# Two sequences' q and k from one projection of 64-row weights, and the mix a pair later beside the output projection

## What is computed

```python
x = x + xattn0(layernorm(x), ctx)   # 8 heads of 8, softmax over |i-j| <= 64,
                                    # y = relu(attention @ w_out) * ctx, then y @ w_ct (the mix)
x = x + ffn0(layernorm(x))          # 256 x 256 ternary weight, scaled, norm clipped
x = x + xattn1(layernorm(x), ctx)   # q from x, k and v from ctx, rotary q and k, full softmax, out projection
x = x + ffn1(layernorm(x))          # 256 -> 1024 -> 256, 4-bit weights with low-rank additions
```

## Time and profile before

| what | value |
|---|---|
| median of 3 runs | 1358.52 us (1356.28 to 1361.82) |
| the profiled execution's own time | 1358.7 us |
| its span, first to last instruction | 1356.8 us |
| mean granted TensorE clock | 0.982 of full speed |
| busy in the span: PE, PEld, DVE, ACT, POOL | 94%, 63%, 68%, 63%, 52% |

### The profile page before, as it was taken

The page is one execution under the profiler, slowest core; times in us unless marked ns, Lnnn a source line. Parts: engine busy times, 40 slices in busy tenths (PEclk is TensorE's granted clock), DMA queues, the critical chain, the costliest instruction groups (busy, mean ns, idle before and its releaser), DMA issues.

```text
span 1356.8 us, 35892 instructions
## 1 busy us (share of the span) xinstructions
PE 1268.8 (94%) x10972; PEld 854.0 (63%) x10972; DVE 927.0 (68%) x2052; ACT 852.3 (63%) x1849; POOL 711.4 (52%) x1297
## 2 busy tenths in 40 slices
PE   6999999999999997868899999999999989999998
PEld 3677667777677764644566556666666646666665
DVE  6788888888888875549999978888888852111110
ACT  2576666666666765555888888888888772222111
POOL 4577778787777865045555656556655410100000
PEclk9999999999999999897999999999999999999999
DMA  8554444544445440023444434444444400000000
GB/s 202 117 132 102 114 113 112 111 109 111 111 102 120 100 96 7 12 52 92 90 99 102 105 88 100 97 102 110 98 97 102 105 6 0 31 16 15 15 15 31
DMA packets 90487, 113.33 MB, mean 84 GB/s; under 512 B 13972, under 2 KB 80276, under 8 KB 82740
## 3 DMA queue, kind: packets, MB, share of 16 engines
q1 hardware_dynamic: 89216, 111.25, 35.3%
q10 hardware_dynamic: 1206, 1.29, 0.4%
HBM read 18.66 MB, written 4.19 MB: 17 GB/s over the span
## 4 chain that ended last, share of the span: by engine, by line
PE 57%; POOL 16%; issue 10%; DVE 9%; ACT 3%; DMA 2%; POOLq 1%; SPq 0%; ACTq 0%; DVEq 0%
PE bank L475 9%; PE bank L435 8%; PE bank L678 8%; PE bank L669 8%; PE bank L451 8%; PE bank L433 5%; PE bank L487 4%; POOL probs L1340 4%; DVE row_max L1118 4%; POOL Qp L1311 2%; POOL rot L1322 2%; PE bank L627 1%; PE bank L507 1%; POOL k_rest L1327 1%; POOL q_rest L1307 1%
## 5 line engine op out<-in xcount | busy, mean ns | idle before, releaser
L1118 DVE TENSOR_REDUCE row_max<-bank 128x2 f32<-128x384 f32 (+1 forms) x1024 | 594.0, 616 | 109.9 <-PE bank L435 105.8
L714 ACT ACTIVATE probs<-bank 128x384 f32<-128x384 f32 (+1 forms) x1024 | 535.1, 542 | 182.9 <-PE bank L451 175.6
L435 PE MATMUL bank<-Ks,Qs 96*128 96x192 bf16 (+1 forms) x2048 | 372.2, 264 | 11.2 <-DMA Ks<-Ks 6.4
L451 PE MATMUL bank<-Qs,Ks 128*128 128x192 bf16 (+1 forms) x2048 | 366.0, 260 | 14.1 <-ACT probs L714 12.9
L1340 POOL TENSOR_SCALAR_AFFINE_SELECT probs<-probs 128x256 f32<-128x256 f32 (+1 forms) x512 | 260.9, 533 | 114.9 <-ACT probs L714 94.5
L435 PEld LDWEIGHTS bank<-Ks,Qs 96*128 96x128 bf16 x2048 | 187.9, 99 | 126.6 <-DVE row_max L1118 32.3
L475 PE MATMUL bank<-probs,V 128*32 128x192 f32 (+1 forms) x4096 | 248.2, 360 | 7.0 <-POOL probs L1340 5.7
L451 PEld LDWEIGHTS bank<-Qs,Ks 128*128 128x128 bf16 x2048 | 185.6, 97 | 48.2 <-ACT probs L714 34.5
L433 PE MATMUL bank<-band,ident 128*128 128x384 bf16 x512 | 168.7, 329 | 3.0 <-DMA Ks<-Ks 2.5
L475 PEld LDWEIGHTS bank<-probs,V 128*32 128x32 f32 x4096 | 107.4, 109 | 85.8 <-issue 43.9
L1277 DVE TENSOR_TENSOR X<-bank,X 128x256 f32 (+1 forms) x32 | 13.6, 424 | 185.6 <-PE bank L678 185.6
(11 more groups left out here) (118 smaller groups left out, 1675.3 us busy)
## 6 DMA issues: line engine op xcount, KB each, us to landing
Ks<-Ks SPq DMA_DIRECT2D x64, 576.0 KB
Qs<-Qs SPq DMA_DIRECT2D x128, 192.0 KB
Qs<-Qp SPq DMA_DIRECT2D x192, 64.0 KB
Ks<-Kp SPq DMA_DIRECT2D x192, 64.0 KB
side<-in_ctx SPq DMA_DIRECT2D x64, 128.0 KB, 2.1
X<-in_x SPq DMA_DIRECT2D x4, 1024.0 KB, 14.5
out<-X SPq DMA_DIRECT2D x8, 512.0 KB, 3.0
Qs<-max_rows SPq DMA_DIRECT2D x128, 12.0 KB
```

What stands on the lines that cost most here:

```text
L435: last = nc.tensor.matmul(dst[:, blk * win:(blk + 1) * win], Qs[0:SHIFT_ROW, pair[1], h, blk * P:(blk + 1) * P], Ks[0:SHIFT_ROW, pair[1], ...
L451: last = nc.tensor.matmul(dst[:, blk * win:(blk + 1) * win], Ks[:, pair[1], h, blk * P:(blk + 1) * P], Qs[:, pair[1], h, start(blk):start( ...
L714: nc.scalar.activation(probs[:, h % 8, 0:2 * win], exp_bank[h % 2][:, 0:2 * win], ACT.Exp, scale=SCALE).then_inc(s["exped"], 1)
L1118: nc.vector.tensor_reduce(row_max[:, pair[1], h, :], bank_of(pair, h)[:, 0:2 * win].rearrange("p (b k) -> p b k", b=2), AX.X, ALU.max).the ...
```

## The change

Both layers get a joined projection of q and k, although only layer 0 has one input for both. The weight has 64 rows (one sequence's channels) and 128 columns, q and k alternating; rows 0 to 63 of the array do the first sequence of the pair into bank A, rows 64 to 127 the second into bank B. Layer 1, whose q comes from xn and k from side, adds two such products with zeros in the other's columns. So bank A holds q and k of one sequence, bank B those of the other, and what follows is by sequence and not by q and k: ScalarE's `high_part` or `turn_rows` of both banks comes at h = 1, VectorE's `rest_of` or `rotate` at h = 1 (A) and h = 2 (B), and GpSimd has one `split` and one `rot_sum` of 512 columns in the place of two of 256. Layer 1's rounding is one 512-wide operation at h = 7. `project_qk` stands at h = 0 on TensorE. In bank B it now precedes max1.

The output projection becomes two products of 64x64 quarters on the diagonal of the array (bank B). Layer 0's mix becomes two products of the off-diagonal quarters into bank A, one pair later (pair r-2), straight behind the output projection at h = 10; ctx is loaded with the two sequences of a pair exchanged, the values' strips are arranged for that, and VectorE's `update` of pair r-2 is at h = 11. The DMAs of the q and k parts take 64 rows of 1 KB in the place of 128 rows of 512 B. The core of the diff:

```diff
 JOBS = {
-    "A": [("q", AHEAD), ("heads", -1), ("v", 2), ("max0", 1)],
-    "B": [("max1", 0), ("k", AHEAD), ("back", -1), ("out", -1), ("mix", -1)],
+    "A": [("qk", AHEAD), ("heads", -1), ("v", 2), ("mix", -2), ("max0", 1)],
+    "B": [("qk", AHEAD), ("max1", 0), ("back", -1), ("out", -1)],
 }
@@ SyncE, lay_out
                 for j in range(PARTS):
-                    dst = bass.AP(q_stack, first + j * row, [[PARTS * row, HD], [T, HPP], [1, T]])
-                    e.dma_start(dst, Qp[:, u, j, :]).then_inc(s[f"q_in{u}"], 16)
+                    dst = bass.AP(q_stack, first + j * row, [[PARTS * row, HD], [2 * T, HEADS], [1, 2 * T]])
+                    e.dma_start(dst, QKp[0:P:2, u, j, :]).then_inc(s[f"q_in{u}"], 16)
@@ TensorE
+            def project_qk(pair):
+                if not active(pair):
+                    return
+                u = pair[1]
+                e.wait_ge(s["xn_ready"], num(pair) + 1)
+                if l:
+                    e.wait_ge(s[f"side_in{u}"], (pair[0] + 1) * 16)
+                wait_bank(e, s, l, "A", "qk", pair)
+                wait_bank(e, s, l, "B", "qk", pair)
+                sources = (xn, side) if l else (xn,)
+                for n, src in enumerate(sources):
+                    last = {}
+                    for bk, rows in (("A", slice(0, CH)), ("B", slice(CH, P))):
+                        last[bk] = nc.tensor.matmul(job_bank[bk][:, 0:T], w[rows, n, :], src[rows, u, :],
+                                                    start=(n == 0), stop=(n == len(sources) - 1))
+                last["A"].then_inc(s["A_filled"], 1)
+                last["B"].then_inc(s["B_filled"], 1)
+            def cross_mix(pair):
+                wait_apart(e, (s["gated"], num(pair) + 1), (s["A_read"], job_order(l, "A", "mix", pair)))
+                for here, there in ((slice(0, CH), slice(CH, P)), (slice(CH, P), slice(0, CH))):
+                    last = nc.tensor.matmul(job_bank["A"][there, 0:T], w[here, MIX, here], gated[here, :],
+                                            start=True, stop=True)
+                last.then_inc(s["A_filled"], 1)
+            def project_out(pair):
+                wait_apart(e, job_wait(s, l, "B", "back", pair, "read"))
+                for here in (slice(0, CH), slice(CH, P)):
+                    last = nc.tensor.matmul(job_bank["B"][here, 0:T], w[here, WO, here], mixed_in[here, :],
+                                            start=True, stop=True)
+                last.then_inc(s["B_filled"], 1)
@@ TensorE, iteration
                     if h == 3:
                         turn_max("B", r, 1)
-                    if h == 1:
-                        project("A", "q", p3, WQ, xn[:, p3[1], :],
-                                lambda: e.wait_ge(s["xn_ready"], num(p3) + 1))
-                    if h == 4 + l:
-                        project("B", "k", p3, WK,
-                                (side if l else xn)[:, p3[1], :],
-                                lambda: l and e.wait_ge(s[f"side_in{p3[1]}"], (p3[0] + 1) * 16))
+                    if h == 0:
+                        project_qk(p3)
                     if h == 10:
-                        project("B", "out", m1, WO, mixed_in[:, :],
-                                lambda: wait_job(e, s, l, "B", "back", m1, "read"))
+                        project_out(m1)
+                    if h == 10 and l == 0:
+                        cross_mix(at(r, -2))
-                    if h == 14 and l == 0:
-                        project("B", "mix", m1, 4, gated,
-                                lambda: e.wait_ge(s["gated"], num(m1) + 1))
@@ ScalarE, iteration
-                    if h == 2 and l == 0:
-                        high_part("A", "q", p3, Qp, 0)
-                    if h == 2 and l == 1:
-                        turn_rows("A", "q", p3, 0, 0)
+                    if h == 1 and l == 0:
+                        high_part(p3)
+                    if h == 1 and l == 1:
+                        turn_rows(p3)
                     if h == 3:
                         max_out("B", r, 1)
...
-                    if h == 4 and l == 0:
-                        high_part("B", "k", p3, Kp, 1)
-                    if h == 5 and l == 1:
-                        turn_rows("B", "k", p3, 1, 1)
-                    if h == 6 and l == 1:
-                        high_part("A", "q", p3, Qp, 0)
-                    if h == 9 and l == 1:
-                        high_part("B", "k", p3, Kp, 1)
+                    if h == 7 and l == 1:
+                        high_part(p3)
@@ VectorE, iteration
-                    if h == (14, 10)[l]:
-                        update(m1)
+                    if h == (11, 10)[l]:
+                        update(m1 if l else at(r, -2))
                     maximum(p1, h)
-                    if h == 2 and l == 1:
-                        rotate("A", "q", p3, 0, 0)
-                    if h == 5 and l == 1:
-                        rotate("B", "k", p3, 1, 1)
-                    if h == 2 and l == 0:
-                        rest_of("A", "q", p3, Qp, q_rest, 0)
-                    if h == 4 and l == 0:
-                        rest_of("B", "k", p3, Kp, k_rest, 1)
+                    if h in (1, 2):
+                        (rotate if l else rest_of)(p3, h - 1)
@@ GpSimd, iteration
                 if l == 0:
                     mask_group(m1, 3)
                     mask_group(r, 0)
-                    split("q", p3, Qp, q_rest, "q_mid", "q_parts")
+                    split(p3)
                     mask_group(r, 1)
-                    split("k", p3, Kp, k_rest, "k_mid", "k_parts")
                     gate(m1)
                     mask_group(r, 2)
                 else:
-                    rot_sum("A", "q", p3, 0, q_rest)
-                    rot_sum("B", "k", p3, 1, k_rest)
-                    split("q", p3, Qp, q_rest, "q_mid", "q_parts")
+                    rot_sum(p3)
+                    split(p3)
                     split_max(e, nc.gpsimd, s, l, p1, 0)
-                    split("k", p3, Kp, k_rest, "k_mid", "k_parts")
                     split_max(e, nc.gpsimd, s, l, p1, 1)
```

More of the change, by code:

```diff
@@ L38, with place_of @@
 COPY_ROW = 72
+def place_of(head, seq):
+    return 2 * (head % 2) + (seq + head // 2) % 2, head // 4
 def at(r, k, ring=RING):
@@ L533, in tensor_attention @@
             tail = {0: lambda: values_group(TAIL, 3), 2: lambda: turn_heads(TAIL), 4: lambda: turn_back(TAIL),
-                    5: lambda: project("B", "out", TAIL, WO, mixed_in[:, :],
-                                       lambda: wait_job(e, s, l, "B", "back", TAIL, "read"))}
+                    5: lambda: project_out(TAIL)}
             if l == 0:
-                tail[8] = lambda: project("B", "mix", TAIL, 4, gated, lambda: e.wait_ge(s["gated"], PAIRS))
+                tail[6] = lambda: cross_mix(at(TAIL, -1))
+                tail[8] = lambda: cross_mix(TAIL)
             def iteration(r, heads=range(HPP)):
@@ L715, in exp_head, with high_part @@
                                      scale=SCALE).then_inc(s["exped"], 1)
-            def high_part(bk, name, pair, parts, column):
+            def high_part(pair):
                 if not active(pair):
@@ L1066, in vector_within @@
         def vector_within(e, n, h):
-            if n == -1 and h == 2:
+            if n == -1 and h == 0:
                 gain_norm(e, 1, FIRST_CHUNK, PAIRS)
@@ L1317, in rot_sum @@
-            def rot_sum(bk, name, pair, n, rest):
+                    wait_apart(e, job_wait(s, l, "A", "qk", pair, "read"), job_wait(s, l, "B", "qk", pair, "read"))
+                    total = 1
+                else:
+                    e.wait_ge(s["qk_high"], n + 1)
+                    nc.gpsimd.tensor_tensor(rest, rest, parts[:, 0, :], ALU.subtract).then_inc(mid, 1)
+                    wait_apart(e, (mid, n * 2 + 1))
+                    total = 2
+                nc.gpsimd.tensor_scalar(parts[:, 1, :], rest, 1.0, None, ALU.mult).then_inc(mid, 1)
@@ L1431, in _layouts @@
     dh = np.arange(CH).reshape(HEADS, HD).T.reshape(-1)
-    packed = np.arange(CH).reshape(2, 4, HD).swapaxes(0, 1).reshape(-1)
+    packed = np.empty((2, 2, 4, 2, HD), int)
+    for half in range(2):
+        for head in range(HEADS):
+            for l in range(2):
+                packed[(l, half, *place_of(head, half if l else 1 - half))] = half * CH + head * HD + np.arange(HD)
+    packed = packed.reshape(2, -1)
     w_in, b_in = f["L0_xattn_w_in"], f["L0_xattn_b_in"]
```

197 lines of the change are left out of this document (100 added, 97 removed).

## The result

Four runs of the changed kernel took 1526.09 to 1527.74 us, median 1527.35; four of the kernel before 1356.28 to 1361.82, median 1358.74. The ratio is 1.124 (95% interval 1.122 to 1.125). The span grew from 1356.8 to 1525.2 us, by 168.4.

What follows compares the result with a forecast made beforehand. TensorE's time and the two turns of the maxima were taken to set the period; 1356.8 + 55 (layer 0) + 71 (layer 1) + 7 (clock) gave 1490 us of span, 1492 us in all, 10% slower, range 1435 to 1540 us.

Steps and rivals of the forecast that it cites:

- the likeliest case: Whole kernel: everything as reckoned, 1492 us, its own range 1450 to 1525 us; chance 66%.
- The mechanism at h = 3, layer 0: Layer 0's turn of the maxima waits for VectorE's second rest, at +4.54 us in place of +2.24, 2.30 us later.
- Products: TensorE: 64-row halves and quarters overlap, each group taking one projection's 0.46 us, plus about 0.11 us per mode change.
- The rival of no overlap: TensorE's row halves run one after another: 1.84 + 0.92 us more per iteration, 80 us, 1572 us; chance 6%.
- the queue in one bank: Quarters at h = 10 writing the same bank can't run together: 13 to 27 us more in layer 0, 1512 us; chance 10%.
- Layer 0's remainder: Behind layer 0's turn: k gone -0.46, heads' wait +0.35, out and mix -0.24; iteration +1.95, taken as 1.9 us.
- The clock: Clock falls behind one wait in four of layer 0, adding 7 us; bounds nothing to 52 to 99 us.
- The 0.35 us for the heads' copy: Layer 0: without k, TensorE waits some 0.35 us for ScalarE's copy of the finished heads.
- the rival of a clock that falls behind most waits: Clock falls behind most waits: 52 to 99 us in place of 7, about 1560 us; chance 10%.
- Layer 1: Turn at h = 3 at 4.9 us, h = 12 at 14.4 behind GpSimd; +2.6 or +2.2 us per iteration, 71 us.
- The gain in TensorE's time of 0.59 us: Layer 0, TensorE: joined projection and quarters sum to 1.25 us against 1.84, gaining 0.59 us per iteration.

Runs made afterwards that it cites:

- e7: Kernel before with only the order changed: k projected at h = 1 ahead of max1 in bank B, its readers at h = 2, nothing joined or quartered; 1473.31 us.
- e2: Changed kernel with the turn of max1 and its copy moved from h = 3 to h = 6 in layer 0 alone; 1450.35 us.
- e1: Changed kernel with 14 idle band matmuls on TensorE in front of layer 0's turn at h = 3, to keep the clock up; 1525.24 us.
- e6: Changed kernel with turns at h = 6, GpSimd's maxima first, row copies apart, layer 0's output and mix at h = 13 behind max0, roundings apart; 1411.96 us.
- e3: Changed kernel with the turn of max1 and its copy moved from h = 3 to h = 6 in both layers; 1449.34 us.
- e4: e3 with GpSimd's split of the maxima (half 0) ahead of the split of q and k; 1424.84 us.

## Why the prediction was right, and where it was too low

1492 us were predicted and 1527.35 measured. Direction and range held; the time was 35 us too low, and 2 us above the 1450 to 1525 that the likeliest case had for itself. The periods were forecast at 17.4 and 17.6 us and came at 18.77 and 17.98. Nearly all the errors go the same way, so the hit isn't one of errors that cancel; the range was wide enough for their sum.

- **The mechanism at h = 3, layer 0: right.** The turn was reckoned at +4.54 us behind the iteration's start and came at 286.63 - 281.90 = +4.73, waiting for VectorE's rest. From the maximum of h = 1 to the end of the second rest it took 1.81 us for 1.80; the signal took 0.30 for 0.15. e7 showed that order alone does it, e2 that moving the turn away takes 77 us back, the clock's share included.
- **Products: right.** Halves and quarters overlap. The joined projection takes 282.54 - 281.90 = 0.64 us for 0.57, the quarters 295.58 - 294.98 = 0.60 for 0.57 without the change of mode on the way in. The rival of no overlap is out. So is the queue in one bank: the two L527 records of 64 rows each, mean 402 ns, take 0.43 us together, in the same bank B. In layer 1, where only bank B is written, all four records of the quarters take 0.65 us (at 1019.06), a single full-width product's two records 0.62. On this point the Trainium skill (TensorEngine Tiling (Array Packing), PSUM Pressure) says that different row tiles can't access the same bank at once; the trace doesn't agree, for quarters that write different partitions of the bank.
- **Layer 0's remainder: the step that failed.** After the turn I gave back 0.35 us (k gone, less for out and mix, a wait for the heads), taking +1.9 for the iteration. It was +3.24, so the part behind the turn cost 0.75 us and not -0.35. With 0.19 us more for the turn itself and the 0.05 rounded off that makes 39 us of error, against which stand the 7 entered for the clock. Two terms were missing or too small, and each alone would fill the 1.1 us behind the turn. One is the clock, below. The other stood at nothing: I had seen that max1 stood behind the joined projection in bank B, and hadn't asked the same of bank A. The mix ahead of max0 puts `update` before the turn at h = 12. e1 shows that wait (1.34 us) when the clock doesn't fall, e2 still has half a microsecond of it, and in e6, where the mix is behind max0, it is gone. The 0.35 us for the heads' copy were 0.25 in e1 and e2, and in the kernel after the slow clock covers them.
- **The clock: right in kind, wrong in number.** I let it fall behind one wait in four, for 7 us. It fell at 25 of layer 0's 32 turns, at every one from 155 to 531 us, for 3.4 us each time, so the rival of a clock that falls behind most waits held for layer 0. In e7, whose waits in layer 0 were 1.8 us long (48.4 in 27) and not 2.4, it fell at 6 of 32. From 288.18 to 291.80 the kernel after needs 3.62 us; e1 needs 291.00 - 288.58 = 2.42 for the same heads, 0.29 us of it a wait for the heads' copy. Twenty-five times 1.2 is 30 us. But it can't be added to the other term: e1 gave the 1.2 us back to TensorE and got nothing, since the wait at h = 12 took 1.34. The two overlap, and each alone looks like the cause.
- **Layer 1: right within its size.** The turn at h = 3 came at 1013.38 - 1008.05 = +5.33 us for 4.9 (1008.05 is 0.22 us behind the last shifted product's start at 1007.83, where the next one would have started at full width; the row copies took the 1.96 us reckoned as 1.9), that at h = 12 at +14.77 for 14.4. GpSimd's wide operations took 1.27, 1.50 and 1.18 us; reckoned were 1.28, 1.5 and 1.18. Per iteration it was +2.92 and +2.50 for 2.6 and 2.2: 80 us for 71. That GpSimd sets the period is shown by e3 (no gain from the turn) and e4 (0.83 us from GpSimd's order). That ScalarE's four row copies also hold up the shifted products (25.0 us in e3) wasn't in the prediction.
- **In the sum:** 94 + 80 - 6 for the ends = 168 us, where I had 55 + 71 + 7 = 133. The 94 hold what the clock cost.
- **The gain in TensorE's time of 0.59 us** isn't in any period. The rows of TensorE give 0.50 of it: 0.64, 0.60 and 0.10 on the way into the quarters, against 1.84. In e6, with both dependencies gone, layer 0 is at its old period, and small waits (0.3 us for the mask, 0.26 for the heads) fill what was saved.

## What to carry to other kernels

Where jobs share a bank in a fixed order, list for every job who reads the one ahead of it and where that read stands in its engine's program; do this for every bank that the change touches, not only for the one in which the first wait was found. A wide operation isn't free because it replaces two: what was behind the second narrow one is now behind the whole, as GpSimd's split was for the maxima. And when two delays of about the same length lie between the same two points, taking away one shows nothing; only taking away both does.

## What the hardware showed that wasn't expected

**Small VectorE operations lasted until the GpSimd operation beside them was over.** The four operations that split the maxima take 0.91 us in the kernel after (294.90 to 295.81, with GpSimd at a mask for 0.43 us of it) and 2.18 in e1 (294.10 to 296.28, GpSimd at its masks and the gate), with the same shapes. GpSimd in e1 at that time:

```profile
293.37 1.59 POOL L1370 TENSOR_SCALAR_AFFINE_SELECT probs<-probs 128x256 f32<-128x256 f32 x3
295.13 0.41 POOL L1370 TENSOR_SCALAR_AFFINE_SELECT probs<-probs 128x256 f32<-128x256 f32 x1 [0.16 <-POOL probs L1370]
295.60 0.73 POOL L1394 TENSOR_TENSOR rot<-rot,side 128x256 f32<-128x256 f32 x1
```

Set beside VectorE's rows of e1 above: the masks end at 294.96, 295.54 and the gate at 296.33; VectorE's operations at 294.44, 295.14 and 295.61 end at 294.99, 295.57 and 296.36, each 0.03 us later. In the kernel after, the one at 295.10 ends at 295.36, the mask beside it (294.91 and 0.43 us) at 295.34. Where GpSimd was idle, the same kinds took 0.16 to 0.18 us. The maxima, which read a bank, took 0.55 us either way. Groups of the whole run, by form, VectorE, after and then e1:

```profile
L1012 DVE TENSOR_TENSOR max_parts<-max_rest,max_parts 128x16 bf16<-128x16 f32 x64 | 13.1, 205 | 2.2
```

```profile
L1017 DVE TENSOR_TENSOR max_parts<-max_rest,max_parts 128x16 bf16<-128x16 f32 x64 | 24.7, 386 | 2.2
```

205 against 386 ns for one; GpSimd's own operations did not get longer (its wide split 1498 and 1510 ns, the gate 730 and 728). This is read from timelines and wasn't tried by itself. It is the likely reason why e1's wait at h = 12 was as long as the clock's cost: with the iteration shifted, VectorE's split fell on GpSimd's masks and the gate.

**The clock stayed low for 3.4 us each time, but didn't fall at the same place.** From 155 to 531 us the iterations of layer 0 alternate. Behind every second wait TensorE ran on at 2.4 GHz for some 1.5 us before the level of 1.2 GHz came; in the iterations between, it came within 0.2 us of the wait's end. At 267.78 and 286.63, one of each, the waits were as good as equal: 2.39 and 2.42 us.
